# Three attention blocks and an MLP in a pipeline: own instruction orders for filling, steady and emptying rounds, all weights set up in the first round, values multiplied over 128 rows

## The reference, cut to what matters

```python
# layer 0
ln = layernorm(x, ln1);  q, k, v = split(ln @ w_qkv + b_qkv)
x1 = x  + attention(q, k, v, ltor_mask) @ w_ao + b_ao        # stage A, self-attention
ln = layernorm(x1, ln2); q = ln @ w_q + b_q;  k, v = split(ctx @ w_kv + b_kv)
x2 = x1 + attention(q, k, v, cross_mask) @ w_co + b_co       # stage B, cross-attention
x3 = x2 + gelu(layernorm(x2, ln3) @ w1 + b1) @ w2 + b2       # stage M, 256 -> 1024 -> 256
# layer 1
a = layernorm(ctx, gamma, beta)
q = x3 @ Wq.T;  k = a @ Wk.T;  v = a @ Wv.T                  # stage C, gated cross-attention
y = x3 + tanh(gate) * (softmax(q k / 4, masked) v) @ Wo.T

def attention(q, k, v, mask):
    s = q k / 4 * mask - 10000 * (1 - mask)
    return softmax(s) @ v
```

## Time and profile before

| | us |
|---|---|
| median of 3 runs | 963.54 (961.01 to 965.07) |
| the profiled execution | 966.05 |
| its span, first to last instruction | 964.3 |
| PE busy | 885.3 (92%) |
| DVE busy | 634.4 (66%) |
| ACT busy | 572.6 (59%) |
| POOL busy | 560.7 (58%) |
| mean granted clock of PE | 0.95 |

### The profile page before, as it was taken

The page is one execution under the profiler, slowest core; times in us unless marked ns, Lnnn a source line. Parts: engine busy times, 40 slices in busy tenths (PEclk is TensorE's granted clock), DMA queues, the critical chain, the costliest instruction groups (busy, mean ns, idle before and its releaser), DMA issues.

```text
span 964.3 us, 30432 instructions
## 1 busy us (share of the span) xinstructions
PE 885.3 (92%) x12880; PEld 839.4 (87%) x12880; DVE 634.4 (66%) x1412; ACT 572.6 (59%) x1073; POOL 560.7 (58%) x565
## 2 busy tenths in 40 slices
PE   5877889999999999999999999999899999998885
PEld 5876889898998999989899989999899999987784
DVE  3564857667685767767586866777686767665533
ACT  4444647557484766758484846758484847655343
POOL 1345666739374674939376664939475765836231
PEclk9577999989998999999999999999999999998987
DMA  6030100100101001010101010010101010010000
GB/s 214 1 106 2 29 15 13 41 13 2 42 14 41 13 25 30 2 53 3 41 12 43 12 42 13 2 53 2 42 13 42 13 42 1 14 31 2 24 13 12
DMA packets 33029, 27.13 MB, mean 28 GB/s; under 512 B 12672, under 2 KB 32000, under 8 KB 32896
## 3 DMA queue, kind: packets, MB, share of 16 engines
q1 hardware_dynamic: 32896, 25.20, 8.8%
HBM read 20.99 MB, written 4.19 MB: 26 GB/s over the span
## 4 chain that ended last, share of the span: by engine, by line
PE 82%; DVE 6%; POOL 4%; issue 3%; ACT 3%; DMA 1%; SPq 0%; DVEq 0%; ACTq 0%; POOLq 0%
PE pj L414 21%; PE pj L432 15%; PE s_bank L497 10%; PE pj L445 10%; PE s_bank L470 10%; PE s_bank L481 9%; PE pj L395 4%; PE pj L510 2%; DVE x L902 1%; POOL prob_B L1112 1%; POOL prob_B L1118 1%; PE pj L374 1%; DVE zT_B_lo L852 1%; ACT zT_B_hi L661 1%; ACT k L705 1%
## 5 line engine op out<-in xcount | busy, mean ns | idle before, releaser
L1098 POOL TENSOR_TENSOR rstd<-var_eps,half 128x2 f32<-128x2 f32 x64 | 47.5, 742 | 242.7 <-DVE var_eps L929 242.7
L705 ACT ACTIVATE k<-pj,kbias,consts 128x256 f32<-128x256 f32 x192 | 93.0, 571 | 49.3 <-PE pj L414 49.3
L1118 POOL TENSOR_TENSOR prob_AC<-prob_AC,rmax_C 128x512 f32<-128x512 f32 x64 | 66.2, 1046 | 90.4 <-DVE rmax_C L883 88.1
L470 PE MATMUL s_bank<-k,q 64*128 64x128 f32 x1536 | 106.7, 282 | 7.8 <-ACT q L692 4.1
L470 PEld LDWEIGHTS s_bank<-k,q 64*128 64x128 f32 x1536 | 91.8, 187 | 19.9 <-ACT q L689 6.4
L1125 POOL TENSOR_TENSOR h_lo<-g,h_hi 128x512 fp32r<-128x512 f32 x64 | 84.5, 1341 | 9.9 <-DVE h_hi L1083 9.9
L1112 POOL TENSOR_TENSOR prob_B<-prob_B,maskB_off 128x512 f32<-128x512 f32 x64 | 81.7, 1299 | 10.9 <-DVE prob_B L878 10.1
L445 PE MATMUL pj<-w_hi_M,h_hi 128*128 128x256 f32 x256 | 80.0, 312 | 4.8 <-issue 3.3
L1112 POOL TENSOR_TENSOR prob_AC<-prob_AC,maskA_off 128x512 f32<-128x512 f32 x64 | 80.6, 1283 | 4.8 <-DVE prob_AC L878 4.8
L713 ACT ACTIVATE prob_AC<-s_bank 128x512 f32<-128x512 f32 x128 | 68.3, 596 | 18.1 <-PE s_bank L481 17.8
L481 PE MATMUL s_bank<-consts,prob_AC 128*128 128x128 f32 x512 | 72.7, 289 | 4.9 <-POOL prob_AC L1118 4.9
(11 more groups left out here) (199 smaller groups left out, 2930.3 us busy)
## 6 DMA issues: line engine op xcount, KB each, us to landing
x_in<-in_x SPq DMA_DIRECT2D x16, 256.0 KB, 2.7
ctx_b<-in_ctx_features SPq DMA_DIRECT2D x16, 256.0 KB, 4.1
ctx_c<-in_ctx SPq DMA_DIRECT2D x16, 256.0 KB, 3.3
out<-y SPq DMA_DIRECT2D x16, 256.0 KB, 2.2
g<-in_w_M SPq DMA_DIRECT2D x2, 1024.0 KB, 7.0
maskB<-in_mask_Bx1xSxS_ff SPq DMA_DIRECT2D x32, 64.0 KB, 3.3
prob_AC<-in_w_A_qkv SPq DMA_DIRECT2D x1, 768.0 KB, 4.5
prob_B<-in_w_B_kv SPq DMA_DIRECT2D x1, 512.0 KB, 5.9
```

The costliest lines, as they stand in the source:

```text
L470: mm = nc.tensor.matmul(bank[:, c, :, b2, :], q2[rows_, c, t * TILE + b2].rearrange("p e q -> p (e q)"), k2[rows_, c, t * TILE + b2], star ...
L705: last = nc.scalar.activation(k2[:, m, :, s, :], k_all[:, m], ACT.Identity, bias=kbias[:, "ABC".index(a), s, m:m + 1], scale=parity[:, 2 + ...
L1118: nc.gpsimd.tensor_tensor(p3, p3, rmax[a][:, r, :].unsqueeze(2).broadcast_to([P, BL * TILE, S]), ALU.subtract).then_inc(shifted[a], 1)
```

## The change

Four things in one edit.

1. **Orders.** Each engine gets eight lists instead of one: `fill0` to `fill3`, `steady`, `drain1` to `drain3`, each written out with its own order. The use of `pj` banks (`PJ_ORDER`) and of score banks (`S_ORDER`) is written out for each kind of round, and the bank count runs on through all rounds instead of starting again in each.
2. **Weights.** 18 pieces with a semaphore each instead of 5 batches. All are loaded in one go ahead of round 1, into more buffers (`z_B`, `z_M`, `xb_M`, `x2`, `o_C`, `ctx_c` besides the old ones). x of unit 0 is loaded first of all. ACT and DVE set the pieces up in rounds 0 and 1; PE waits for a piece where it first uses it. The shift matmuls of B stand in round 1 between two `turn_probs`, those of M_1 and of C at the start of rounds 2 and 3, in a `pj` bank of their own.
3. **Values.** `vz` gets an axis for the sequence and holds zeros for the other sequence: rows of sequence 0 have their values in columns 0 to 16 and zeros in 17 to 33, rows of sequence 1 the other way round. A matmul takes all 128 rows and 34 moving columns. The copy becomes two of 64 rows. A and C share one `vz`, so a copy waits for the other stage's sums.
4. **Buffers.** `xb_B` is now `x1` itself: POOL adds the bias in place, behind the layernorm of x1. `xb_A` waits for the token addition of the unit before. `rden` is one buffer.

Core of the diff:

```diff
-PJ = ["C.xT", "C.K", "A.zT", "C.Q", "B.V", "M.zT", "B.zT", "B.K", "B.Q", "M.H1", "M.H0", "M.H2", "A.K",
-      "A.Q", "M.H3", "A.V", "C.OT", "M.cT", "M.Y0", "C.AO", "B.OT", "M.V", "B.AO", "A.OT", "M.Y1", "A.AO"]
+PJ_ORDER = {
+    "fill1": ["P.cA", "A.zT", "A.K", "A.Q", "A.V", "P.cB", "A.OT", "A.AO"],
...
+    "steady": ["C.xT", "C.K", "A.zT", "C.Q", "B.V", "M.zT", "B.zT", "B.K", "B.Q", "M.H0", "M.H1", "M.H2",
+        "A.K", "M.H3", "A.Q", "A.V", "C.OT", "M.cT", "M.Y0", "C.AO", "B.OT", "M.V", "B.AO", "A.OT", "M.Y1",
+        "A.AO"],
...
-def pj_bank(name):
-    return PJ.index(name) % PJ_BANKS
+PJ_AT = {n: k for k, n in enumerate([n for n in in_order(PJ_ORDER) if active(n[0][0], n[1])])}
+def pj_bank(name, i):
+    return PJ_AT[name, i] % PJ_BANKS
...
-        vz = {a: sb(f"vz_{a}", [P, T, 2, NPAIR, VW]) for a in "ABC"}
+        vz = {"B": sb("vz_B", [P, T, 2, NPAIR, TILE, VW]), "A": sb("vz_AC", [P, T, 2, NPAIR, TILE, VW])}
+        vz["C"] = vz["A"]
...
-                        for b2 in range(TILE):
-                            rows_ = slice(b2 * S, (b2 + 1) * S)
-                            mm = nc.tensor.matmul(
-                                s_banks[e * S:(e + 1) * S, t * HALVES + b2, m * VW:(m + 1) * VW],
-                                prob[a][rows_, t * HALVES + half, n, e * S:(e + 1) * S],
-                                vz[a][rows_, t, e, m, :], start=True, stop=True)
+                        mm = nc.tensor.matmul(
+                            s_bank[t * HALVES][e * S:(e + 1) * S, m * TILE * VW:(m + 1) * TILE * VW],
+                            prob[a][:, t * HALVES + half, n, e * S:(e + 1) * S],
+                            vz[a][:, t, e, m, :, :].rearrange("p b v -> p (b v)"), start=True, stop=True)
...
+                for b2 in range(TILE):
+                    half = slice(b2 * S, (b2 + 1) * S)
+                    last = nc.vector.tensor_copy(
+                        vz[a][half, :, :, :, b2, 0:HD].rearrange("p t e m v -> p (t e m) v"),
+                        pj[pj_bank(name, i)][half, :].rearrange("p (n f) -> p n f", f=HD))
...
+            body(0)
             sp.dma_start(consts[:, :], d["constants"]).then_inc(const_in, 16)
-            load(0)
-            body(0)
+            load(("A.K", "A.Q", "A.V"))
             rest(...)
-            load(1)
-            load(2)
-            load(3)
-            body(1)
-            body(2)
-            sp.wait_ge(setup_lo, pieces_until(3))
-            load(4)
-            run(sp, body, 3, LAST)
+            load(("A.AO", "B.V", "B.K", "B.Q", "B.AO", "M.H0", "M.H2"))
+            load(("M.V", "M.Y0a0", "M.Y0a", "M.Y0b0", "M.Y0b", "C.K", "C.Q", "C.AO"))
+            run(sp, body, 1, LAST)
```

The steady order changes in places. On PE (`steady`, against `body`):

```diff
                     token_major("B.V", i)
-                    scores("C", 0, i)
                     turn("M.zT", z["M"], i)
+                    scores("C", 0, i)
                     scores("C", 1, i)
...
+                    feature_major("M.H0", i)
                     feature_major("M.H1", i)
-                    feature_major("M.H0", i)
                     scores("B", 0, i)
+                    scores("B", 1, i)
                     feature_major("M.H2", i)
-                    scores("B", 1, i)
                     turn_probs("C", 0, i)
                     feature_major("A.K", i)
+                    feature_major("M.H3", i)
...
                     values("C", 1, i)
-                    feature_major("M.H3", i)
                     token_major("A.V", i)
```

More of the change, by code:

```diff
@@ L385, in claim, with carry_shifts @@
                 if not isinstance(n, int) or n:
-                    pe.wait_ge(pj_free[pj_bank(name)], n)
-                return pj[pj_bank(name)]
+                    pe.wait_ge(pj_free[pj_bank(name, i)], n)
+                return pj[pj_bank(name, i)]
+            def carry_shifts(l, i):
+                name = f"P.c{l}"
+                bank = claim(name, i)
+                at = SHIFT_AT[l]
+                for use in SHIFTED[l]:
+                    n = PIECE[use]
+                    pe.wait_ge(weights_in[n], 16)
+                    w = PIECES[n][3]
+                    shift = lnvec[:, LN[l], 1, :]
+                    for m in range((PIECES[n][7] - PIECES[n][6]) // P):
+                        for k in range(KC):
+                            last = nc.tensor.matmul(bank[:, at:at + 1], w[:, k, m * P:(m + 1) * P], shift[:, k:k + 1],
+                                                    start=(k == 0), stop=(k == KC - 1))
+                        at += 1
+                last.then_inc(pj_full[pj_bank(name, i)], 1)
             def turn(name, src, i):
@@ new lines, in drain3 @@
+            def drain3(i):
+                pe.wait_ge(tokens["M"], T * (unit("C", i) + 1))
+                turn("C.xT", x3, i)
+                feature_major("C.K", i)
+                feature_major("C.Q", i)
+                scores("C", 0, i)
+                scores("C", 1, i)
+                turn_probs("C", 0, i)
+                turn_probs("C", 1, i)
+                turn_probs("C", 2, i)
+                turn_probs("C", 3, i)
+                values("C", 0, i)
+                values("C", 1, i)
+                turn_out("C", i)
+                token_major("C.AO", i)
@@ new lines, in body @@
+            def body(i):
+                if i == 0:
+                    fill0(i)
+                elif i == 1:
+                    fill1(i)
+                elif i == 2:
+                    fill2(i)
+                elif i == 3:
+                    fill3(i)
+                elif i <= U:
+                    steady(i)
+                elif i == U + 1:
+                    drain1(i)
+                elif i == U + 2:
+                    drain2(i)
+                else:
+                    drain3(i)
@@ new lines, in drain3, with body @@
+            def drain3(i):
+                high_part("C.xT", i, ("C.Q", i - 1))
+                keys("C", i)
+                queries("C", i)
+                exps("C", 0, i)
+                exps("C", 1, i)
+                exps("C", 2, i)
+                exps("C", 3, i)
+                high_part("C.OT", i, ("A.AO", i - 1), BV["C"])
+            def body(i):
+                if i == 0:
+                    fill0(i)
+                elif i == 1:
+                    fill1(i)
+                elif i == 2:
+                    fill2(i)
+                elif i == 3:
+                    fill3(i)
+                elif i <= U:
+                    steady(i)
+                elif i == U + 1:
+                    drain1(i)
+                elif i == U + 2:
+                    drain2(i)
+                else:
+                    drain3(i)
@@ L847, in low_part @@
                 dve.wait_ge(hi_done[name], unit(name[0], i) + 1)
[L848 removed]
+                bank = pj[pj_bank(name, i)]
                 hi, lo = OP[name]
```

1267 lines of the change are left out of this document (1001 added, 266 removed).

## The result

The changed kernel takes 922.62 us, median of 4 runs (921.54 to 923.51), against 964.31 (961.01 to 968.12) for the kernel before: ratio 0.957, 95% interval 0.953 to 0.960. Forecast were 910 us, with 882 to 942 as the range. It is faster by 42 us, where 54 were forecast.

What follows compares the result with a forecast made beforehand. TensorE was taken to bound the steady rounds, chains of waits the filling and emptying. 964.3 - 31 (steady) - 14 (filling) - 9 (emptying) gave a 910 us span, 912 as profiled execution, and 910 as median forecast; range 882 to 942.

Steps and rivals of the forecast that it cites:

- The stops: Steady rounds, TensorE at values matmuls: waits for the next 256 instructions, all taken as gone, -15.9 us.
- The low clock of 12.3 us: Steady rounds: work done at a lower clock, expected to go with the stops, -12.3 us.
- Values at 0 for TensorE: Values blocks: half as many matmuls over 128 rows take the same time, 0 us; bounds -45 and +88.
- rivals 1: The 48 values blocks: column halves load one after the other, 3.7 us a block, +88 us, 998 us; chance 0.06.
- 2 (about 1): Values blocks: cost goes by instruction, a block falls to 0.93 us, -45 us, 865 us; chance 0.07.
- Steady rounds, -31 forecast: The 13 steady rounds: -15.9 stops, -12.3 clock, -7.7 wait before C.K, +4.9 new orders; 52.0 us a round.
- 0.35 us a round: Steady rounds: allowance for new waits from doubled copies, shared buffers and moved moments, 4.9 us in all.
- the bank count: Steady rounds: running count gives C.K another bank, so its 0.59 us wait for A.AO's addition goes, -7.7 us.
- rival 3: Steady rounds: new TensorE waits, such as for zT_B_lo behind doubled copies, +20 to 26 us, 933 us; chance 0.17.
- The filling, -14 forecast: Filling rounds: earlier weights and new orders, turn of z_B at about 50.5 us, -14 us; bounds +10 and -31.
- the 9 us of idle time: Rounds two and three: 9 of 11.8 and 6.1 us TensorE idle, with the clock, saved by interleaving by need.
- The emptying, -9 forecast: Emptying rounds: order and bank count remove stops such as 1.86 us for B.AO's bank, -9 us; bounds 0 and -20.

Runs made afterwards that it cites:

- the values alone: Kernel before with only values over 128 rows (with its buffers and shared vz), old orders, banks and weights: 950.72 us, ratio 0.985.
- all but the values: Kernel after with values back over 64 rows, its new orders, banks, weights and buffers kept: 932.51 us, ratio 0.965.
- the best kernel: Kernel after with C normalised ahead of high_h, M and C shifts one round ahead, A.OT's split part and A's normalising earlier in filling only: 912.01 us.
- the last two kernels: Kernel after with C's normalising and shifts moved, plus A.OT's split part and A's normalising earlier: with steady rounds included 919.39 us, filling only 912.01.

## Why the prediction came out as it did

**The stops: right.** 15.1 us in steady rounds are gone, the instruction queue moves 79 packets, the border of 256 was shown by moving it, and the packets end 1.3 to 1.5 us ahead of each stop's end. Two readings were off: of the "15.6 us in 11 stops" at the values line two (2.3 us) are those of the emptying rounds, which don't follow the count, and the 15.9 us of the sum hold 0.8 of small gaps. The low clock of 12.3 us went too, with the values alone as well. But it wasn't the stops' doing alone, as the kernel with new orders and old values shows.

**Values at 0 for TensorE: right.** 2.06 us with half the records. That alone puts rivals 1 (3.7 us) and 2 (about 1) out; the earlier trace rows, with the period of a matmul of one moving column, had made them unlikely. (Their prices were loosely added: 1.8 x 48 is 86 us, and a block that falls to 0.93 us would give -54, not -45.)

**Steady rounds, -31 forecast, -28.5 measured: right in sum, by two errors that cancel.** "For all of these together I put back 0.35 us a round": it is 1.16 (0.87 for o_C, 0.29 for oT_AC_lo), 15.1 us instead of 4.9. Against that TensorE is busy 20.9 us less, not 12.3; of the other 8.6 most lie in the scores, whose halves now run back to back (87.1 us in the steady rounds before and with the values alone, 80.2 after and with all but the values), and some in the bank count, priced at 7.7 us and worth 10.5. New waits came, as rival 3 said, but zT_B_lo, its example, isn't among those of the kernel after. The wait for o_C is not there in the kernel before, nor with the values alone, though VectorE has a high_h between the two halves of C there too: it comes with the new orders. TensorE had M.H3 and A.V between the last values of C and the turn of o_C (2.95 us), and now has A.V alone, since M.H3 moved ahead. The kernel before, TensorE (its M.H3 and its turn), then VectorE:

```profile
502.13 0.39 PE L414 MATMUL pj<-zT_M_hi,w_hi_M 128*128 128x256 f32 x1
505.08 0.60 PE L510 MATMUL pj<-consts,o_C 128*128 128x128 f32 x4
...
502.73 1.11 DVE L1083 CAST h_hi<-g 128x512 fp32r<-128x512 f32 x1
504.04 0.42 DVE L894 TENSOR_TENSOR o_C<-s_bank,rden_C 128x256 f32<-128x256 f32 x1
```

The second half is ready at 504.46 us there, 0.6 before TensorE wants it. VectorE and then GpSimd in the changed kernel (start, us), where TensorE is done with A.V at 486.5 and the second half is ready at 487.33:

```profile
484.28 0.42 DVE L1303 TENSOR_TENSOR o_C<-s_bank,rden 128x256 f32<-128x256 f32 x1
485.16 1.55 DVE L1798 CAST h_hi<-g 128x512 fp32r<-128x512 f32 x1 [0.46 <-ACT g L965]
486.63 0.24 DVE L1301 RECIPROCAL rden<-s_bank 128x16 f32<-128x16 f32 x1
...
485.14 1.29 POOL L1840 TENSOR_TENSOR h_lo<-g,h_hi 128x512 fp32r<-128x512 f32 x1
...
L1798 DVE CAST h_hi<-g x64: 412/428/1570, 106.8 to 887.7; 128x512 fp32r<-128x512 f32 x64
```

The copy that stands between the two halves takes 0.43 us at the median and 1.55 where GpSimd started 0.02 us before it; it ends 0.28 us after GpSimd does. The run that put it behind the second half took the wait away; M.H3 back in its old place was not tried.

**The filling, -14 forecast, +1.2 measured: the step that failed.** It was "M's come (3.5 us warm)" and the turn of z_B "to about 50.5", and behind it the 9 us of idle time. The timeline after:

```profile
43.91 6.82 PE L423 MATMUL pj<-consts,g 128*128 128x1 f32 x32
50.59 0.56 PE L475 MATMUL pj<-w_hi_B_kv,cT_B_hi 128*128 128x256 f32 x1
...
53.30 1.05 PE L434 MATMUL pj<-consts,z_A 128*128 128x128 f32 x4
54.15 1.06 PE L434 MATMUL pj<-consts,z_B 128*128 128x128 f32 x4
```

The turn of z_A came at 53.30 us, 3.5 later than before, that of z_B at 54.15, 0.8 earlier. TensorE was busy 12 of 20 us ahead of the shifts, and the clock had fallen from 1.00 to 0.61 in the mean (windows):

```profile
24.00:43.90 19.90, 12.16 (x104) 10.54 (x105) 14.58 (x36) 10.92 (x22) 9.02 (x10) 0.61 0.00 1
12.00:24.00 12.00, 8.74 (x71) 7.94 (x69) 7.40 (x17) 7.64 (x16) 0.81 (x1) 1.00 0.95 312
```

At 1.2 GHz (a granted clock of 0.50 from 43.91 to 53.30 us) the shifts took 6.8 us and B.V behind them 2.7, in the chain itself. The earlier trace rows had the same 32 matmuls at 5.75 us, at a granted clock of 0.62; I took a warm price for a place behind waits. That explains 3 to 4 us, by the run that moved them. Of the 9 us of idle time that the second and third round were to give, they gave 2 (94.3 us from the turn of z_A to the first steady round before, 92.0 after; 90.7 in the best kernel). In the whole filling after, TensorE's longest waits behind the one for the first weights are for GpSimd (5.7 us), q (5.4) and oT_AC_lo (5.3), the chain of scores, softmax and split parts. What of it another order could take away was not tried beyond the last two kernels.

**The emptying, -9 forecast, -16.5 measured: mis-sized.** The bound of -20 held. With the values alone it takes 109.1 us, with all but the values 96.85: orders and banks did it, and 4.9 us of that is the bank count, which the prediction named and priced too low. The other 11 to 12 us were not taken apart.

**The sum, -54 forecast, -43.8 of span measured.** The 15 us missing in the filling were half made good by the emptying, which is luck: the two terms have nothing to do with each other.

## What to carry to other kernels

Split idle time and low clock by mechanism and place before pricing an order: the steady rounds came out within 3 us, while the filling, priced as a share of its idle time, gave nothing. Price a moved piece at the clock of its new place. And when an instruction moves back in a queue, look at everything queued behind it, not only at its own reader: here the additions behind z_M's moments in VectorE's queue turned a gain of 3.8 us into a loss. Look too at what covered a wait: M.H3, moved ahead, had hidden the second half of o_C.

## What the runs showed of the hardware

- The count of TensorE's instructions can cost time by itself: with twice the records in the same 2.06 us of values, TensorE stopped for 0.7 to 2.2 us at one border of 256 in seven or so (11 between 190 and 844 us before), although the work was the same. It went on 1.3 to 1.5 us after the packet with the next 256 had ended.
- VectorE's copy of 128 x 512 from SBUF to SBUF waited for GpSimd's subtraction (`h_lo`): 0.43 us at the median, 1.55 beside one that started 0.02 us before it, with its end 0.28 us behind GpSimd's. The Trainium skill (SBUF — State Buffer, "SBUF: two separate sides") calls the port pair that the two can share an exclusive lock, held for a whole instruction; the rows above agree.
- The granted clock differs between executions of the same work, and the chains at both ends show it. Between 24 and 48 us two kernels with the same first round had 0.66 and 0.54, and the second turned z_A for its next round 4.0 us later (both waited 2.6 us for cT_B_lo ahead of it); and the last round took 24.70 us at 0.84 in the kernel after, 27.90 at 0.71 in that with the shifts moved:

```profile
24.00:48.00 24.00, 16.60 (x143) 14.69 (x144) 18.48 (x47) 10.89 (x23) 10.27 (x13) 0.66 0.00 1
```

```profile
24.00:48.00 24.00, 18.04 (x134) 16.37 (x134) 16.08 (x39) 10.81 (x22) 9.44 (x10) 0.54 0.00 1
```

```profile
893.00:920.90 27.90, 16.84 (x159) 14.40 (x157) 9.95 (x18) 8.31 (x14) 4.09 (x4) 0.71 0.03 10
```

(The last row is the emptying round; its clock is 0.71.) A filling or emptying edit worth 3 us needs several runs, or the comparison of one stretch at one clock.
